# High and low halves of the gated values two steps behind the silus, down products four steps behind

## The reference, cut to what matters

```python
h1 = jax.nn.silu(jnp.einsum('th,eih->eti', x, w_gate))   # 160 experts, INTER = 64
h1w = h1 * combine.T[:, :, None]
routed = jnp.einsum('eti,ehi->th', h1w, w_down)
shared = jax.nn.silu(x @ w_gate_shared.T) @ w_down_shared.T
x = x + gb * (routed + shared)
```

## Time and profile before

| what | us |
|---|---|
| median of 3 runs | 712.17 |
| lowest and highest | 712.03, 716.12 |
| the profiled execution, its own time | 714.16 |
| its span, first to last instruction | 711.7 |
| TensorE busy | 597.3 |
| VectorE busy | 481.7 |
| ScalarE busy | 428.7 |

### The profile page before, as it was taken

One profiled execution on the slowest core, in us unless ns is written; L12 is line 12 of the kernel. 1 busy time (PEld: TensorE's weight loads), 2 busy tenths in 40 slices (PEclk: granted clock), 3 DMA queues, 4 the chain that ended last, 5 costly groups with the idle time before them and its releaser, 6 DMA issues.

```text
span 711.7 us, 7473 instructions
## 1 busy us (share of the span) xinstructions
PE 597.3 (84%) x2610; PEld 256.5 (36%) x2610; DVE 481.7 (68%) x624; ACT 428.7 (60%) x682; POOL 29.0 (4%) x57
## 2 busy tenths in 40 slices
PE   3997998878778899998878899998878787777775
PEld 2543443423233344443333344443323333333332
DVE  4754468987887755578687745578686666666664
ACT  4254566778777655466777645466776565555553
POOL 6011000010000000001000000001000000000000
PEclk9999999999999999999999999999999999999999
DMA  8930163444354443344344432344335444444440
GB/s 295 410 145 1 32 224 118 148 134 133 118 160 150 153 134 107 100 148 149 128 137 167 149 127 96 119 143 153 118 129 180 149 159 156 148 149 147 149 147 15
DMA packets 32263, 101.81 MB, mean 143 GB/s; under 512 B 3426, under 2 KB 8035, under 8 KB 31971
## 3 DMA queue, kind: packets, MB, share of 16 engines
q1 hardware_dynamic: 32226, 101.35, 42.1%
HBM read 98.97 MB, written 2.36 MB: 142 GB/s over the span
## 4 chain that ended last, share of the span: by engine, by line
PE 30%; DVE 25%; ACT 21%; issue 21%; POOL 1%; DMA 0%; ACTq 0%; DVEq 0%; SPq 0%; POOLq 0%
DVE s_all L901 19%; ACT g_all L621 15%; PE bank L924 8%; PE bank L926 7%; PE bank L925 7%; DVE g_all L897 3%; ACT s_all L602 2%; PE bank L1051 2%; ACT t L566 1%; ACT L602 1%; PE bank L1127 1%; DVE w L755 1%; ACT L569 1%; DVE key L875 1%; POOL c_all L423 0%
## 5 line engine op out<-in xcount | busy, mean ns | idle before, releaser
L897 DVE TENSOR_TENSOR g_all<-s_all,g_all 128x1024 f16<-128x1024 f32 x160 | 196.0, 1225 | 173.4 <-ACT g_all L621 173.1
L621 ACT ACTIVATE g_all<-s_all 128x1024 f16<-128x1024 f32 x160 | 168.9, 1056 | 157.1 <-DVE s_all L901 156.9
L602 ACT ACTIVATE s_all<-bank 128x512 f32<-128x512 f32 x320 | 178.7, 586 | 72.2 <-PE bank L926 72.1
L901 DVE TENSOR_TENSOR s_all<-s_all,c_all 128x1024 f32<-128x1024 f32 x160 | 195.0, 1219 | 6.1 <-DMA c_all<-combine 3.7
L924 PE MATMUL bank<-x_h,w 128*128 128x512 f16 x320 | 122.9, 384 | 79.5 <-ACT s_all L602 79.2
L924 PE MATMUL bank<-g_all,w 128*128 128x512 f16 x320 | 121.6, 380 | 3.5 <-DVE g_all L897 3.5
L925 PE MATMUL bank<-g_all,w 128*128 128x512 f16 x320 | 121.5, 380 | 0.0
L926 PE MATMUL bank<-g_all,w 128*128 128x512 f16 x320 | 121.5, 380 | 0.0
L926 PE MATMUL bank<-x_l,w 128*128 128x512 f16 x320 | 121.5, 380 | 0.0
L925 PE MATMUL bank<-x_h,w 128*128 128x512 f16 x320 | 121.5, 380 | 0.0
L924 PEld LDWEIGHTS bank<-x_h,w 128*128 128x128 f16 x320 | 31.0, 97 | 167.5 <-ACT s_all L602 144.5
(11 more groups left out here) (196 smaller groups left out, 432.3 us busy)
## 6 DMA issues: line engine op xcount, KB each, us to landing
c_all<-combine SPq DMA_DIRECT2D x160, 512.0 KB, 3.8
w<-w_dram SPq DMA_DIRECT2D x20, 512.0 KB, 12.4
s_all<-mats_dram SPq DMA_DIRECT2D x1, 1152.0 KB, 6.9
attw<-symT_dram SPq DMA_DIRECT2D x1, 1152.0 KB, 10.0
res<-x_dram SPq DMA_DIRECT2D x4, 256.0 KB, 9.7
combine<-cT SPq DMA_DIRECT2D x4, 256.0 KB, 4.2
out_dram<-res SPq DMA_DIRECT2D x4, 256.0 KB, 2.4
g_all<-wmod_dram SPq DMA_DIRECT2D x1, 384.0 KB, 3.6
```

The source lines that it names most:

```text
L602: a(sr[J % SRING][:, q * L:(q + 1) * L], U[q][:], ACT.Silu, scale=1.0 / ES).then_inc(s["s_done"], 1)
L621: a(gh[n % GRING], sr[n % SRING], ACT.Copy).then_inc(s["hi_set"], 1)
L897: e.tensor_tensor(gl[n % GRING], sr[n % SRING], gh[n % GRING], ALU.subtract).then_inc(s["lo_set"], 1)
L901: e.tensor_tensor(sr[J % SRING], sr[J % SRING], cr[J % CRING], ALU.mult).then_inc(s["gm"], 1)
```

## The change

`HOLD = 2` is new: ScalarE's high half at step J is that of n = J - 2, and VectorE's low half too. `LAG` goes from 3 to 4: TensorE's down products at step J are those of J - 4, and the end of a chunk comes one step later. Rings keep their sizes. The loop's tail has four steps in place of three. In the setup pieces 3 and 4 are moved from behind `setup(9)` to behind `att(0, "h2a")`.

```diff
-LAG = 3
+HOLD = 2
+LAG = 4
@@ walk
     att(0, "o1")
     setup(9)
-    piece(3, 5)
     att(1, "turn")
     att(0, "x2")
     att(1, "hnT")
...
     att(0, "h2m")
     att(0, "h2a")
+    piece(3, 5)
     att(1, "conv0c")
     att(0, "turn2")
@@ scalar, duo(J)
-                if 1 <= J <= ALL:
-                    n = J - 1
+                n = J - HOLD
+                if 0 <= n < ALL:
                     act.wait_ge(s["gm"], n + 1)
```

## The result

The changed kernel takes 622.14 us (median of 4 runs, 620.57 to 623.70), the kernel before 712.82 in the same runs. The ratio is 0.872, with a 95% interval of 0.868 to 0.876. The forecast was 619, range 603 to 645. The profiled execution of `hold2_lag3` took 1211.75 us, its 128x512 matmuls starting 0.44 us apart although the granted clock is on record as 1.00 throughout, so what is read of that kernel comes from its other executions and from a second profile, `hold2_lag3_again`.

A forecast was written before the change was run, and what follows sets the result against it. A 3.48 us ring between VectorE and ScalarE was taken to bound each duo. Seven stretch terms, 98.0 + 85.5 + 35.9 + 142.1 + 141.6 + 104.9 + 10.1, gave a 618.1 us span and a forecast of 619, range 603 to 645.

The forecast's parts named there:

- The ring: In the duo loop, product, high half, low half and next duo's product wait for each other: 3.48 us a duo.
- TensorE at 2.60 is next: With the halves two steps behind, TensorE's 12 matmuls at 0.2165 us bound a duo at 2.60 us.
- The third rival: TensorE goes faster than 0.2165 us a matmul, so VectorE at 2.28 bounds a duo: 587 us, chance 0.01.
- LAG = 4: Down products: three steps behind, the low half is ready at +1.1, wanted at 0.65; the fourth step avoids this wait.
- the layout: One duo timed from its first up product's start; the silu's need for an earlier low half has 2.3 us to spare.
- The combine loads: Loads for VectorE's product: issued at -5.6, landing 3.8 us later, wanted at 3.6; at least 2.5 us stay.
- The pieces: Setup: moving two weight pieces lets `hnT` be copied earlier and may end slow matmuls; bounds 0 and 3.5, value 3.0 us.
- the first term: Start up to duo 3: 101.87 us less 3.0 for the setup and 0.9 for the first high half, 98.0.
- Duos 3 to 27: Chunk 0 beside weight pieces and mixer: VectorE's work of 81 and 4.5 for ScalarE's table loads, 85.5 us, from 97.4.
- Chunk 1: TensorE's real work of 137.8 us plus 4.3 for waits that stay: 142.1 us, from 159.6.
- The fifth rival: TensorE gets the lower clock while working without a pause: a duo takes 5.2 us, the whole 786, chance 0.03.
- The mutual waits of 157 and 173 us: ScalarE's high half waiting for VectorE's product, and VectorE's low half for the high half: both down to some tens.

The follow-up runs named there:

- hold2_lag3: The changed kernel with LAG put back from 4 to 3, HOLD still 2: 664.09 us; run again for a second profile as hold2_lag3_again, 665.25 us.
- hold1_lag4: The changed kernel with HOLD put back from 2 to 1, LAG still 4 and the pieces moved: 719.47 us, ratio to the kernel before 1.010.
- the one-more and one-less pair: The changed kernel with a fourth matmul in each up product, 672.41 us, and with one of each three taken away, 588.52 us.
- loads_late: The changed kernel with three buffers for the combine weights in place of four, each load issued one duo later: 622.04 us.

## Why the prediction was right

- **The ring.** It was read as product, high half, low half, next product, 3.48 us. `hold1_lag4` keeps the ring and keeps the 3.48; HOLD = 2 opens it. Shown.
- **TensorE at 2.60 is next.** 2.59 measured in chunk 3; the one-more and one-less pair shows that it is TensorE and by how little VectorE comes behind it (2.27). The third rival's bound for VectorE, 2.28, was right, its premise (a faster matmul) was not.
- **LAG = 4.** The low half ready at +1.1 and wanted at +0.65 was the reason given for the fourth step. It is worth more than that reckoning suggests, 42 us of the 91, because the wait that it keeps away is longer where mixer items lie beside the duos. One number of the layout contradicts itself: the low half of J - 4 ends 1.5 us ahead of the duo's start, not 2.2; the 2.3 us to spare come from the 1.5 and are right.
- **The combine loads.** The 2.5 us of slack that I gave them held: one duo later changed nothing.
- **The pieces.** 3.0 forecast with bounds of 0 and 3.5; 3.5 measured, both parts of it (the earlier copy and the stretch at half pace). That pace did not return at this place in the changed kernel. The early setup was 0.5 us shorter in its trace (transposes of chunk 1 at 61.89, 62.39 before), which is half of the 1.0 by which the first term came out better than forecast.
- **The stretches.** Five of seven terms were within about 1 us. Three came out up to 1.0 too high and three 0.7 to 2.7 too low, so that the span missed by 3.1 where the low ones alone would have made it 5.7: a part of the closeness is luck. The term "Duos 3 to 27" was 2.7 short: VectorE's work was right (81.10 busy beside my 81), but its idle time was 7.1, not 4.5, and its busy share 0.92, not over 0.93. Two waits behind ScalarE's table loads are 2.23 and 1.92 of it, and one of 1.56 at 104.35, where TensorE's mixer matmuls still lead, I had not counted. The first of them, in the changed kernel and in `loads_late`:

```profile
158.80 1.23 DVE L898 TENSOR_TENSOR g_all<-s_all,g_all 128x1024 f16<-128x1024 f32 x1 [2.23 <-ACT g_all L622]
157.23 1.22 DVE L898 TENSOR_TENSOR g_all<-s_all,g_all 128x1024 f16<-128x1024 f32 x1 [1.27 <-ACT g_all L622]
```

It is 0.96 us longer in the changed kernel, and nearly all other periods of the two traces agree to 0.01. The changed kernel's granted clock was at the 1.2 GHz level from 140.69 to 144.10, behind two waits of TensorE of 1.81 and 2.19 us; that of `loads_late` stayed at the 2.4 GHz level through the loop. So about 1 of the 2.7 us goes with a low stretch that the term did not hold, and not with the table loads. "Chunk 1" was 2.3 short: the 4.3 us left for waits were too few (1.3 at the copy of Y, 0.8 at the shared expert, 1.1 at a low half, 2.3 at silus, 0.2 at the combine weights, and the drain at each, make 6.7), but the 1.1 and most of the 2.3 were not in my list.
- **The clock.** The fifth rival did not come: granted 0.98 to 1.00 in all stretches, and 1.00 in the densest one, chunk 3 with TensorE 99% busy. The one low stretch of the changed kernel's loop stood, like those before, behind waits and not behind dense work.
- **A sign that missed.** The mutual waits of 157 and 173 us were to fall to some tens: 4.9 and 90.8 are left. The second goes back to TensorE only by way of ScalarE's order.

## What to carry to other kernels

When two engines' idle times name each other, write down the ring of their instructions, its length, and over how many steps of the loop it reaches; if it is longer than the busiest engine's work, one more step of distance can be worth the difference. It needs ring buffers to reach over; here those at hand sufficed. Then check every consumer behind the delayed value in the same way: here the consumer needed its own extra step, each of the two lags alone gave half or nothing, and with the buffers as they were one of them met a second ring. Once an engine is near 99% busy, only the places where it stands idle by program order are left, and turning two items round at such a place gave 4 us where a deeper ring gave none.

## What the hardware showed that was not expected

- One wait of TensorE in a pipeline with slack does not cost each duo the same: in `hold2_lag3_again` the periods alternate 2.60 and 3.12, with the mean of the reckoned ring (2.86 beside 2.85).
- VectorE ran 39 duos in 90.03 us with 89.34 busy, while 220 GB/s of loads landed in the same memory and ScalarE and TensorE read it: its two instructions took 1.21 us each, as elsewhere (1.22). No contention between them was seen at that rate.
